# Local layers: the bank that the product of V is written to

## The reference

```
h = shift_token(x)
q, k, v = split(h @ wqkv, 3, axis=-1)             # 8 heads of 64
q, k = l2norm(q) * qs, l2norm(k) * ksc
q, k = rotary_xpos(q, k)                          # two products by tables, one with the halves turned
# each window of 64 tokens looks at itself and the window before
sim = einsum('bhwid,bhwjd->bhwij', bq * 8, look_around(bk)); masked
o = einsum('bhwij,bhwjd->bhwid', softmax(sim), look_around(bv))
x = x + o @ wo
h = layernorm(shift_token(x)) * lg + lb
a, g = split(h @ w1 + b1, 2, axis=-1)
x = x + (a * gelu(g)) @ w2 + b2
```

## Time and profile before

| | us |
|---|---|
| median of 3 runs | 2137.15 (2135.57 to 2139.05) |
| the profiled execution, its own time | 2139.61 |
| its span, first to last instruction | 2137.9 |
| busy PE | 1770.4 (83%) |
| busy DVE | 1354.6 (63%) |
| busy ACT | 1167.6 (55%) |
| busy POOL | 893.4 (42%) |

### The profile page before, as it was taken

One profiled execution on the slowest core, in us unless ns is written; L12 is line 12 of the kernel. 1 busy time (PEld: TensorE's weight loads), 2 busy tenths in 40 slices (PEclk: granted clock), 3 DMA queues, 4 the chain that ended last, 5 costly groups with the idle time before them and its releaser, 6 DMA issues. The chain is left out here.

```text
span 2137.9 us, 41383 instructions
## 1 busy us (share of the span) xinstructions
PE 1770.4 (83%) x12676; PEld 915.7 (43%) x12676; DVE 1354.6 (63%) x2378; ACT 1167.6 (55%) x2826; POOL 893.4 (42%) x1047
## 2 busy tenths in 40 slices
PE   7559999967168673999999965699999999999996
PEld 4324444425157461232333313355555555555552
DVE  5646777722212443788888813578788888878872
ACT  2226676641023241677777740477767777767771
POOL 5424544531410651011111111567666676666660
PEclk9759999986579785899999985799999999999996
DMA  4312222210033121122222221011111111111110
GB/s 128 111 47 80 74 78 86 73 55 2 29 108 90 47 81 62 52 85 76 81 86 80 78 91 62 23 34 37 38 32 36 45 40 37 33 38 33 47 36 13
DMA packets 93685, 126.53 MB, mean 59 GB/s; under 512 B 17041, under 2 KB 56852, under 8 KB 93457
## 3 DMA queue, kind: packets, MB, share of 16 engines
q1 hardware_dynamic: 91536, 121.11, 17.9%
q0 software_dynamic: 2048, 4.16, 0.7%
HBM read 66.28 MB, written 43.52 MB: 51 GB/s over the span
## 5 line engine op out<-in xcount | busy, mean ns | idle before, releaser
L1025 DVE TENSOR_REDUCE M_sb<-banks 128x1 f32<-128x512 f32 (+3 forms) x1024 | 539.8, 584 | 201.0 <-PE banks L825 114.9
L911 ACT ACTIVATE probs_sb<-banks 128x512 f32<-128x512 f32 (+3 forms) x1024 | 469.1, 521 | 195.7 <-PE banks L851 192.0
L822 PE MATMUL banks<-K_sb,Q_sb 72*128 72x512 bf16 (+3 forms) x1024 | 360.4, 358 | 67.7 <-PEq L344 57.9
L851 PE MATMUL banks<-Q_sb,K_sb 75*128 75x512 bf16 (+3 forms) x1024 | 345.8, 345 | 8.1 <-DMA Q_sb<-mrows_sb 4.1
L866 PE MATMUL banks<-probs_sb,V_sb 128*32 128x512 f32 (+3 forms) x2048 | 234.5, 529 | 11.8 <-issue 7.7
L822 PEld LDWEIGHTS banks<-K_sb,Q_sb 72*128 72x128 bf16 x1024 | 100.7, 99 | 319.5 <-DVE M_sb L1025 172.5
L1820 ACT ACTIVATE l_p_sb<-banks,l_nb_sb,l_inv_sb 128x128 f32<-128x128 f32 x512 | 228.0, 465 | 12.9 <-DVE l_nb_sb L1992 12.7
L1906 POOL TENSOR_TENSOR l_pn_sb<-l_p_sb,l_rs_sb 128x512 f32<-128x512 f32 x128 | 150.1, 1172 | 149.6 <-DVE l_rs_sb L1998 148.1
L1898 POOL TENSOR_TENSOR l_inv_sb<-l_clip_sb,l_minus_half_sb 128x16 f32<-128x16 f32 x64 | 186.2, 2910 | 57.1 <-DVE l_clip_sb L1967 55.2
L1891 POOL TENSOR_TENSOR l_ts_sb<-l_t_sb 128x1024 f32<-128x1024 f32 x64 | 153.3, 2395 | 32.6 <-DVE l_kn_sb L1976 16.9
L851 PEld LDWEIGHTS banks<-Q_sb,K_sb 75*128 75x128 bf16 x1024 | 100.0, 99 | 96.1 <-ACT probs_sb L911 21.3
(11 more groups left out here) (202 smaller groups left out, 3356.7 us busy)
## 6 DMA issues: line engine op xcount, KB each, us to landing
Q_sb<-qk_dram SPq DMA_DIRECT2D x192, 96.0 KB
o_dram<-osum_sb SPq DMA_DIRECT2D x64, 256.0 KB, 4.9
l_vs_sb<-l_vt_sb SPq DMA_DIRECT2D x112, 128.0 KB, 2.3
qk_dram<-parts_sb SPq DMA_DIRECT2D x96, 128.0 KB
K_sb<-qk_dram SPq DMA_DIRECT2D x32, 288.0 KB
opack_sb<-o_dram SPq DMA_DIRECT2D x16, 256.0 KB, 3.4
inverse_sb<-s_dram SPq DMA_DIRECT2D x16, 256.0 KB, 3.3
ew_sb<-in_ew SPq DMA_DIRECT2D x16, 256.0 KB, 3.5
```

Source lines behind the costliest of these rows:

```text
L822: mm = pe.matmul(out[:, 0:width], g.Q[0:RK, slot, h, k * P:(k + 1) * P], g.K[0:RK, slot, hk(h), 0:width], start=True, stop=not causal)
L851: pe.matmul(SB[ring % 3][:, t0:N], g.K[0:RM, q, hk(h), k * P:(k + 1) * P], g.Q[0:RM, q, h, t0:N], start=True, stop=True).then_inc(s["b_sco ...
L911: act.activation(g.probs[:, k, h, t0:N], SB[ring % 3][:, t0:N], ACT.Exp, scale=scale)\
L1025: dve.reduce_max(g.M[:, u % 2, k, h:h + 1], SA[ring % 3][:, 0:width], AX.X, negate=True)\
```

## The change

The product of V goes to bank 2, the bank of the turned probabilities, and no longer to bank 4. With that, project no longer waits for the copy of V, values no longer waits for the rotation of tile t+2 but for ACT's copies of the turned probabilities of tile t-1 (which pv, just ahead of it, waits for too), and turn(t, 0) now waits for the copy of V of tile t. In PE's order values moves ahead of gate 2 (t = 2) and value 2 (t = 3); at t = 0 and 1 it stays where it was. The orders of DVE, ACT, POOL and SP stay as they are. Lines behind the edits move up by one to three.

```
-    SB, TB, OB, QK, VB, XB, YB = g.pair[0], g.bank[2], g.bank[3], g.pair[2], g.bank[4], g.bank[6], g.bank[7]
+    SB, TB, OB, QK, VB, XB, YB = g.pair[0], g.bank[2], g.bank[3], g.pair[2], g.bank[2], g.bank[6], g.bank[7]
...
                 pe.wait_ge(s["t1"], it * CH + a)
                 pe.wait_ge(s["t2"], it * 2 * CH + 2 * a)
-                if a > 2 or not isinstance(it, int) or it:
-                    pe.wait_ge(s["v"], it * CH + a - 2)
                 for w in range(2):
...
-            def values(it, a, layer, projected):
+            def values(it, a, layer):
                 c = a % CH
-                pe.wait_ge(s["t1"], it * CH + projected)
-                pe.wait_ge(s["t2"], it * 2 * CH + 2 * projected)
+                pe.wait_ge(s["pt"], it * 2 * CH + 2 * a)
                 pe.matmul(VB[:, :], g.xs[:, c * P:(c + 1) * P], g.lw[:, layer, 2 * INNER:3 * INNER],
...
             def turn(it, t, e):
                 pe.wait_ge(s["pnorm"], it * 2 * CH + 2 * t + e + 1)
                 pe.wait_ge(s["pt"], it * 2 * CH + 2 * t + e)
+                if e == 0:
+                    pe.wait_ge(s["v"], it * CH + t + 1)
...
                     if earlier:
                         pv(it, t - 1)
+                    values(it, t, layer_of(it, new))
                     if t == 2 and age:
                         gate(it, 2, old)
                     if t == 3 and age:
                         value(it, 2, old)
-                    values(it, t, layer_of(it, new), t + 3 if ahead else CH)
```

## The result

The changed kernel takes **2156.41 us** (median of 4 runs, 2154.48 to 2159.65) against 2136.36 for the kernel before (4 runs, 2135.45 to 2139.05): the ratio is 1.0093, 95% interval 1.0076 to 1.0111, so 20.05 us slower. The forecast was 2161.0 within 2147 to 2176. The profiled execution took 2156.66 us, its span is 2154.4. Lines of the kernel after stand 1 to 3 higher up than in before: project is L1624, values L1631, turn L1671, gate L1719, on DVE the copy of V L1982 and the row maxima L1987.

A forecast was written before the change was run, and what follows sets the result against it. The prediction took a chain of waits from project through the scores to DVE's row maxima as the bound, with no engine full. Its terms, 11.4 + 13.4 - 1.0 = 23.8 us on the median 2137.15, gave 2161.0 us, range 2147 to 2176.

The forecast's parts named there:

- What bounds the kernel: Local layers: a chain through project and the scores into DVE's row maxima; delaying project by x delays the maxima by x.
- The waits removed: V's product no longer waits for the rotation: no gain in middle batches, 1.0 us once in batch 0.
- Tile 1 to 2: The turn waits for the copy of V and starts 0.88 us later, in 13 batches: 11.4 us.
- Tile 2 to 3: V's product ahead of gate 2 delays the third gate step, copy and turn by 0.96 us, in 14 batches: 13.4 us.
- The other two passages: From tile 3 to 0 and tile 0 to 1 the change gives no gain and no cost.
- Sum: All terms together: 11.4 + 13.4 - 1.0 = 23.8 us slower.
- Both passages cost: The forecast case: tile 1 to 2 and tile 2 to 3 both lose time, 2154 to 2167 us; chance 0.62.
- one passage: Rival: only one of tile 1 to 2 and tile 2 to 3 costs, 2145 to 2154 us; chance 0.11.
- nothing: Rival: the moved wait for v meets unseen slack, time 2137 within a few microseconds; chance 0.06.
- The clock: Rival: PE's clock falls from tile 1 to 2 in a third of the batches or more, 2167 to 2182 us; chance 0.16.
- Faster: Rival: the 26.7 us of rotation waits leave the path, 2110 us, or 2124 for about half; chance 0.05.

The follow-up runs named there:

- the wait alone: The kernel before, V still in bank 4, with only one wait added: turn of the even heads also waits for the copy of V; 2163.99 us, ratio 1.0112.
- the order undone: The changed kernel with values put back behind gate 2 and value 2, bank and waits kept; 2160.01 us, ratio 1.0101.
- the early copy: The changed kernel with the copy of V moved ahead of repeat_deviation and the third gate step in DVE's order; 2132.25 us, ratio 0.9971.
- early copy with the old bank: The kernel before, V in bank 4, with the copy of V moved to the same early places in DVE's order; 2168.82 us, ratio 1.0152.

## Why the prediction was right

- *What bounds the kernel.* Right. A delay of project came out at the maxima: in batch 7, counted from the maxima before it, project starts 0.90 later from tile 1 to 2 and 0.96 from 2 to 3, and the next maxima come 0.83 and 0.93 later; the sum of these distances is the loss.
- *The waits removed.* Right: all gone, and they gave nothing in the batches in the middle. turn_item, ahead of the turn, waits 0.66 us for kn there. For batch 0 I had 1.0 within 0 to 2.08; it was 0.8, and 0.3 more in batch 1. The turn met POOL, as I had put it, and started 5.37 us after the maxima of tile 0 in place of 6.54; but the clock then fell, and project took 3.58 us in place of 2.82.
- *Tile 1 to 2.* 0.88 a batch expected, 0.83 measured. The turn was released by the copy of V, as expected, and started 0.14 us behind it in place of my 0.05. The copy itself came at the same place in DVE's order and no earlier. I had counted batches 1 and 4 at nothing; they gained 0.5 to 0.6 each, since their fall of the clock went. V's product now runs in the gap that stood ahead of it, but that this is the reason is not shown: with the wait alone the gap is as before, and batch 1 had no fall there either. With 0.61 in the last batch, the term was 9.4 in place of 11.4.
- *Tile 2 to 3.* 0.96 expected, 0.86 to 0.93 measured, and the chain was the one written: V's product, gate 2, DVE's third gate step, copy, turn. The last batch I took at nothing because no project stands behind its turn. Its maxima came 0.89 later too, since the scores stand behind that turn, but the turn of the last tile did not: it is held by POOL, 16.61 and 16.65 us after the maxima of tile 2. So in the total the term of nothing held, by another way than I gave. The run with the order undone splits the step of the other batches: 0.32 to 0.40 for the wait, near the 0.35 that I had as the lower bound, and the rest for V's product ahead of gate 2.
- *The other two passages.* Tile 0 to 1 cost nothing. Tile 3 to 0 cost 0.1 us in most batches, 1.0 us, which I had not seen. In batch 2 the whole of it lies between the end of POOL's probabilities and the turn, 0.24 us in place of 0.13; why stays open.
- *Sum.* 23.8 expected; the local layers grew by 22.6. Against it stand 2.3 us behind the last maxima: the 0.9 of the last batch, and 1.4 from the clock, which I had no term for. That leaves 20.3; the medians differ by 20.05.
- *The rivals.* Both passages cost, which rules out *one passage* and *nothing*. The clock: in the changed kernel it did not fall at tile 1 to 2, in no batch, although PE pauses 1.21 us ahead of the turn. But in its near relations it did: in seven batches with the wait alone, 0.6 to 0.8 us each, and in four with values behind gate 2, 1.6 to 1.7 in three of them; I had priced a fall at 1.41. So it deserved its chance. The Trainium skill, "TensorE: Matmul & The Clock Gate", section "HAM oscillation — how this bites in real kernels", describes such a fall between bursts; the runs agree that it happens, in some turns of a loop and not in every one. *Faster* named the point from which it decides, that the copy end before POOL's probabilities: the kernel with the early copy does just that, and is faster.
- *A reason I gave and would not give again.* "DVE's order is unchanged and the copy had no idle time before it there, so I see no room." There was room: about 0.6 us of c_spread's 1.26 (1.26 against 0.67 with the early copy) were a wait inside an instruction that the trace counts as busy.

## What to carry to other kernels

A buffer that two users share orders their work; here, when one of them moved to a buffer that had a user already, the wait did not go but was laid on that other user. So ask where the reader that frees the new buffer stands in its engine's order, and what the newly waiting engine has queued behind the wait: here it cost 0.8 to 0.9 us, twice a batch. And measure such a move together with the orders that the old sharing had fixed: here it was 0.9% slower alone, and 0.8% faster with one step moved in DVE's order and one in PE's.

## What the runs showed of the hardware

**A copy of DVE that waits while it counts as busy.** c_spread, a copy of 128x512 f32 from SBUF to SBUF, by kernel (all 16 in the local layers; busy us, mean ns), in the order changed kernel, early copy, early copy with the old bank:

```profile
L2023 DVE COPY c_spread_sb<-c_rs_sb 128x512 f32<-128x512 f32 x16 | 19.4, 1212 | 1.1 <-POOL c_rs_sb L1912 1.1
...
L2023 DVE COPY c_spread_sb<-c_rs_sb 128x512 f32<-128x512 f32 x16 | 10.4, 651 | 1.1 <-POOL c_rs_sb L1912 1.1
...
L2024 DVE COPY c_spread_sb<-c_rs_sb 128x512 f32<-128x512 f32 x16 | 31.1, 1942 | 1.1 <-POOL c_rs_sb L1913 1.1
```

In 15 of the 16 of each kernel it ran into an instruction of POOL that had begun before it, and ended 0.28 to 0.29 us behind that one, whether it had taken 0.67, 1.26 or 2.33 us. The sixteenth found POOL idle and took 0.43. V's copy, which reads PSUM, took 0.67 to 0.69 throughout, with POOL at work or not. The Trainium skill, "SBUF — State Buffer", section "Who interferes with whom", says that a copy can take up a pair of ports which DVE shares with GpSimd, that whichever issues first has the pair for its whole instruction, and that a DVE instruction with at most one SBUF input does not contend outside the modes that use both ports. The three kernels agree for c_spread, which came second each time; V's copy has no SBUF input and was not held.

**PE's clock hangs on little.** The same stretch, tile 1 to 2 of 15 batches, fell to the lower level in 2 (before), 0 (changed), 7 (the wait alone), 4 (values behind gate 2) and 0 (the same with one more product of V in the gap). In the two executions of the kernel with values behind gate 2, three of the four batches are the same. Ahead of a fall PE had done short products and paused for 0.7 to 1.9 us, but the same pauses pass without a fall in the neighbouring batch. What tells batch 8 from batch 7 there stays open.
